# Attention scores in 32-row tiles, without a copy of the keys by head

## The chip, the cores and the metric

One core of a Trainium2 chip runs the whole kernel in one launch. The metric is the device time in microseconds of that core.

## What is computed

A two-layer decoder on x (4 sequences, 256 tokens, width 128) with a context of the same shape. After every block comes a residual add and a layer norm:

```
x = layernorm(x + self_attention_0(x))        # 16 heads of 8, rope, biases
x = layernorm(x + cross_attention_0(x, ctx))  # 16 heads of 8, biases
x = layernorm(x + mixture_0(x))               # 8 experts, all run, gate of the top 2
x = layernorm(x + causal_1(x))                # one head of width 128
x = layernorm(x + cross_attention_1(x, ctx))  # 16 heads of 8
x = layernorm(x + mixture_1(x))               # 8 experts, top 1, capacity 128
# an attention block with heads:
scores = einsum('bhqd,bhkd->bhqk', Q, K) * scale
out    = einsum('bhqk,bhkd->bhqd', softmax(scores), V) @ Wo.T + bo
```

The change touches the three blocks with 16 heads.

## The kernel before

Each sequence is a program of steps, written with `yield`. Two lanes (sequences 0, 2 and 1, 3) take turns step by step, lane 0 ahead by `LAG` = 16 steps (`take_turns`). Every engine runs the same two programs in the same turns, so the order on each engine is fixed when the kernel is built. A block with heads has a few steps of projection, 25 steps of heads (`HEAD_STEPS`), three steps at its end (`attention_end`) and three of normalisation. While one lane is in the early steps of its heads the other is in its late ones; while a lane is in the middle, the other is between two blocks. PSUM's eight banks are four pools of two, S, E, C and M, which both lanes share; `bank_turns` walks the same steps and gives each use its bank, and the helpers `wait_free`, `wait_filled` and `wait_drained` wait on the counters of that bank.

Heads have width 8. For float32r matmuls (`f32r`) Q and K are split in a high and a low part and spread out by matmuls with 0/1 matrices (`spread_rows`, L609 and L611), so that head 4t+g takes 32 partitions, 32g to 32g+31, of column block t in `q_sp` and `k_sp`. A contraction over these 32 rows gives that head's scores. Before, the contraction runs over all 128 partitions: `k_head` holds the keys of one head in its 32 partitions and zeros elsewhere. SP fills it by DMA from `k_sp`, four DMAs for each half of the heads (L543), into a buffer that POOL zeroed at the start (L460, L511); `k_sp` itself lies in the last two slots of `expo`.

One head k passes through these steps of `heads`:

- step k, PE L675: two matmuls of scores into a bank of S; DVE L1171 takes the negated maximum into `negmax`.
- four heads at a time, at step 4t+5 (`SHIFT_AT`), PE L661 transposes `negmax` into a bank of M and DVE L1166 adds it to the queries: `q_sh`.
- step k+7 (`EXP_AT`), PE L687: two matmuls of the shifted scores, keys on the partitions, into a bank of E; ACT L953 takes the exponential into one of six slots of `expo`.
- PE L703 multiplies the values of a group of four heads, each into 32 partitions of one bank of C, in two halves of the keys: the first at step 4t+11, the second at step 4t+12 (`VALUES_AT`). ACT L958 copies the bank out at step 4t+12, behind the exponential of that step. An f32 matmul is two passes on PE, so four heads are eight passes in a half.

`attention_end` transposes the contexts back (L717) when the last copy is done; DVE divides by the sums (L1182, L1183), PE transposes again (L726) and projects (L738), and the layer norm follows. The mixture (L797 to L809) uses `expo` for its hidden values.

Of the kernel before, what the change touches and what calls it, by code (L numbers as in the profile page):

```python
# [36 lines left out]
P = 128  # L37
BATCH, SEQ = 4, 256
TOKENS = BATCH * SEQ
TILES = TOKENS // P  # L40
QT = SEQ // P
# [7 lines left out]
ESLOTS = 6  # L49
# [66 lines left out]
def bank_turns():  # L116
# [4 lines left out]
    def steps(seq):  # L121
# [144 lines left out]
def decoder(nc, ins, out):  # L266
# [3 lines left out]
    with stack:  # L270
# [48 lines left out]
        def lanes(name, shape, dt=f32):  # L319
# [9 lines left out]
        k_head = lanes("k_head", [P, GROUPS, 4, SEQ], f32r)  # L329
# [40 lines left out]
        v_zeroed, lane1_zeroed = sem("v_zeroed"), sem("lane1_zeroed")  # L370
# [6 lines left out]
        k_head_ready = [[sem(f"k_head_ready{i}_{half}") for half in range(2)] for i in range(BATCH)]  # L377
# [55 lines left out]
        with nc.Block() as block:  # L433
# [25 lines left out]
            def _(pool):  # L459
                nc.gpsimd.memset(k_head[0][:].bitcast(u32), 0)  # L460
# [19 lines left out]
        with nc.Block() as block:  # L480
            @block.gpsimd
            def _(pool):
# [26 lines left out]
                nc.gpsimd.memset(v_aug[1][:].bitcast(u32), 0).then_inc(v_zeroed, 1)  # L509
                nc.gpsimd.memset(negmax[1][:].bitcast(u32), 0)  # L510
                nc.gpsimd.memset(k_head[1][:].bitcast(u32), 0)  # L511
                pool.wait_ge(v_zeroed, 2)
# [20 lines left out]
            def _(sp):  # L533
                def by_head(seq, b, what):

                    half = int(what[2])
                    wait_drained(sp, seq, b, what)
                    if seq == 1:
                        sp.wait_ge(lane1_zeroed, 1)
                    t = slice(2 * half, 2 * half + 2)  # L540
                    for g in range(4):
                        r = slice(32 * g, 32 * g + 32)
                        sp.dma_start(k_head[seq][r, t, g, :].bitcast(f32),  # L543
                                     k_sp[seq][r, t, :].bitcast(f32)
                                     ).then_inc(k_head_ready[seq][half], 16)

# [3 lines left out]
                for seq, b, what in TURNS:  # L550
                    if what in ("sk0", "sk1"):
                        by_head(seq, b, what)
                    elif b == SELF0 and seq < LANES and what[0] == "pv":
# [28 lines left out]
            def _(pe):  # L582
# [69 lines left out]

                def heads(seq, b):
                    for k in range(HEAD_STEPS):
# [10 lines left out]
                        if k < HEADS:  # L665
                            t, g = k // 4, k % 4
                            if k == 0:
                                wait_drained(pe, seq, b, "sq0")
                                pe.wait_ge(k_head_ready[seq][0], 64 * (MHA[b] + 1))
                            if k == 8:  # L670
                                wait_drained(pe, seq, b, "sq1")
                                pe.wait_ge(k_head_ready[seq][1], 64 * (MHA[b] + 1))
                            wait_free(pe, seq, b, ("max", k))
                            for qt in range(QT):
                                last = mm(where(seq, b, ("max", k))[:, qt * SEQ:(qt + 1) * SEQ],  # L675
                                          q_sp[seq][:, t, qt * P:(qt + 1) * P],
                                          k_head[seq][:, t, g, :],
                                          start=True, stop=True)
                            last.then_inc(full(seq, b, ("max", k)), 1)
                        if 0 <= k - EXP_AT < HEADS:  # L680
                            h = k - EXP_AT
                            t, g = h // 4, h % 4
                            if g == 0:
                                wait_drained(pe, seq, b, ("shift", t))
                            wait_free(pe, seq, b, ("exp", h))
                            for kt in range(QT):
                                last = mm(where(seq, b, ("exp", h))[:, kt * SEQ:(kt + 1) * SEQ],  # L687
                                          k_head[seq][:, t, g, kt * P:(kt + 1) * P],
                                          q_sh[seq][:, t, :],
                                          start=True, stop=True)  # L690
                            last.then_inc(full(seq, b, ("exp", h)), 1)
                        for kt in range(QT):
                            t = group_at(k, VALUES_AT - 1 + kt)
                            if t is None:
                                continue
                            if kt == 0:
                                wait_drained(pe, seq, b, ("exp", 4 * t + 3))
                                wait_free(pe, seq, b, ("pv", t))
                                if t == 0:
                                    wait_drained(pe, seq, b, "v")  # L700
                            for g in range(4):
                                h = 4 * t + g
                                last = mm(where(seq, b, ("pv", t))[32 * g:32 * g + 32, 0:SEQ],  # L703
# [918 lines left out]
```

## Time and profile before

| what | value |
|---|---|
| median of 3 runs | 496.33 us |
| lowest, highest | 494.31, 496.59 us |
| span of the profiled execution, first to last instruction | 492.2 us |
| PE busy | 420.9 us, 86% of the span |
| DVE busy | 311.8 us, 63% |
| ACT busy | 235.1 us, 48% |
| POOL busy | 48.6 us, 10% |
| chain that ended last | PE 64%, DVE 21%, ACT 7%, issue 4% |

The profile gives the profiled execution's span and no time of its own beside it; the three runs lie 2.1 to 4.4 us above that span. PE is TensorE's matmul, PEld its weight load, DVE VectorE, ACT ScalarE, POOL GpSimd, SP SyncE. Matmuls are pipelined: a single one of 256 columns lasts some 280 ns, but a row of them advances faster, which is why the chain of waits is the view for what a matmul costs in a stream.

### The profile page before, as it was taken

The page shows a single profiled execution, that of the slowest core. Times are in us where ns is not written, and L with a number is a line of the kernel's source. Part 1 is how long each engine was busy: PE and PEld are TensorE (multiplying, and loading weights), DVE is VectorE, ACT ScalarE, POOL GpSimd, SP SyncE. Part 2 cuts the span into 40 slices and gives each one's busy share as a digit, 9 for nine tenths or more (in the row PEclk, how much of TensorE's full clock was granted, in tenths as well). Part 3 has the DMA queues.
Part 4 walks back from the last instruction along what each step waited for, and adds up shares of the span by engine and source line. Part 5 has one row for each costly group of instructions (what it writes and reads, how often), then busy time and mean ns, then how long its engine had stood idle before and what let it go on. Part 6 is the DMA issues. An engine that isn't in the chain of part 4 may idle for free.

```text
span 492.2 us, 9126 instructions
## 1 busy us (share of the span) xinstructions
PE 420.9 (86%) x3332; PEld 340.0 (69%) x3332; DVE 311.8 (63%) x916; ACT 235.1 (48%) x527; POOL 48.6 (10%) x56
## 2 busy tenths in 40 slices
PE   3589898999999978998798989999999969984393
PEld 2476666668999966675766766668999956652292
DVE  3686766673555678685867667754755577763534
ACT  2147656663334326654255757572433437571131
POOL 6200282000000000002020000000000000010114
PEclk9889999999999999999789999999999989998588
DMA  8403323600010010002010201000010042060301
GB/s 282 142 25 89 78 72 96 161 1 1 2 31 14 2 43 1 1 3 53 1 37 16 45 1 43 1 1 2 1 43 3 1 132 82 1 182 1 95 7 34
DMA packets 18906, 22.52 MB, mean 46 GB/s; under 512 B 2984, under 2 KB 13361, under 8 KB 18864
## 3 DMA queue, kind: packets, MB, share of 16 engines
q1 hardware_dynamic: 17344, 18.68, 14.3%
q10 hardware_dynamic: 1008, 2.31, 1.4%
q0 software_dynamic: 512, 0.97, 0.6%
q8 instruction: 27, 0.44, 0.4%
q14 instruction: 15, 0.12, 0.1%
HBM read 13.63 MB, written 2.11 MB: 32 GB/s over the span
## 4 chain that ended last, share of the span: by engine, by line
PE 64%; DVE 21%; ACT 7%; issue 4%; DMA 1%; SPq 0%; POOLq 0%; POOL 0%; DVEq 0%; ACTq 0%
PE bank_C L809 12%; PE bank_S L675 8%; PE bank_C L703 7%; PE bank_E L687 7%; DVE negmax L1171 5%; PE bank_M L609 3%; ACT expo L953 2%; PE bank_M L738 2%; PE bank_M L611 2%; PE bank_E L797 2%; PE bank_S L797 2%; PE bank_M L661 2%; PE bank_E L799 2%; PE bank_E L798 2%; DVE x_rows L1219 1%
## 5 line engine op out<-in xcount | busy, mean ns | idle before, releaser
L1171 DVE TENSOR_REDUCE negmax<-bank_S 128x2 f32<-128x512 f32 x192 | 128.4, 685 | 50.3 <-PE bank_S L675 50.1
L953 ACT ACTIVATE expo<-bank_E 128x512 f32<-128x512 f32 x192 | 113.5, 597 | 83.5 <-PE bank_E L687 82.3
L675 PE MATMUL bank_S<-k_head,q_sp 128*128 128x256 f32 x384 | 97.0, 338 | 10.7 <-DVE negmax L1171 7.2
L675 PEld LDWEIGHTS bank_S<-k_head,q_sp 128*128 128x128 f32 x384 | 61.5, 199 | 39.1 <-issue 25.0
L687 PE MATMUL bank_E<-q_sh,k_head 128*128 128x256 f32 x384 | 81.3, 294 | 0.7 <-DVE q_sh L1166 0.5
L703 PE MATMUL bank_C<-expo,v_aug 128*32 128x256 f32 x768 | 61.5, 393 | 4.6 <-ACT expo L953 4.6
L687 PEld LDWEIGHTS bank_E<-q_sh,k_head 128*128 128x128 f32 x384 | 60.3, 194 | 6.5 <-issue 3.5
L809 PE MATMUL bank_C<-mix_w,expo 128*128 128x128 f32 x512 | 62.5, 275 | 0.7 <-issue 0.7
L809 PEld LDWEIGHTS bank_C<-mix_w,expo 128*128 128x128 f32 x512 | 59.9, 192 | 1.1 <-issue 1.1
L1014 ACT ACTIVATE expo<-bank_S,b 128x256 f32<-128x256 f32 x64 | 26.8, 470 | 53.6 <-PE bank_S L799 53.2
L1276 DVE TENSOR_SCALAR expo<-bank_E,b 128x256 f32<-128x256 f32 x64 | 27.9, 477 | 28.1 <-PE bank_E L799 28.0
L486 POOL TENSOR_TENSOR xb<-x_rows,rows 128x256 f32<-128x256 f32 x12 | 8.4, 706 | 320.6 <-DVE x_rows L1219 318.1
L1287 DVE SCALAR_TENSOR_TENSOR y<-bank_C,g_w,y 128x128 f32<-128x128 f32 x64 | 19.4, 345 | 25.3 <-PE bank_C L809 25.3
L609 PE MATMUL bank_M<-qk_hi,spread 128*128 128x256 f32 x96 | 26.3, 306 | 10.4 <-DVE qk_lo L1110 5.3
L609 PEld LDWEIGHTS bank_M<-qk_hi,spread 128*128 128x128 f32 x96 | 18.1, 188 | 16.4 <-DVE qk_lo L1110 10.7
L703 PEld LDWEIGHTS bank_C<-expo,v_aug 128*32 128x32 f32 x768 | 15.2, 108 | 18.3 <-ACT expo L953 6.6
L912 ACT ACTIVATE expo<-bank_M,const 128x512 fp32r<-128x512 f32 x24 | 15.4, 684 | 19.4 <-PE bank_M L611 19.4
L611 PE MATMUL bank_M<-qk_lo,spread 128*128 128x256 f32 x96 | 24.1, 281 | 0.0
L661 PE MATMUL bank_M<-const,negmax 128*128 128x128 f32 x96 | 20.0, 291 | 1.5 <-DVE ctx_n L1183 1.3
L797 PE MATMUL bank_S<-qk_hi,w_hi 128*128 128x256 f32 x64 | 20.6, 322 | 0.0
L1166 DVE TENSOR_TENSOR q_sh<-q_sp,bank_M 128x256 fp32r<-128x256 f32 x48 | 19.8, 413 | 1.0 <-PE bank_M L661 1.0
L958 ACT ACTIVATE ctx_sb<-bank_C 128x256 f32<-128x256 f32 x48 | 18.6, 387 | 3.9 <-PE bank_C L703 3.8
(185 smaller groups left out, 654.7 us busy)
## 6 DMA issues: line engine op xcount, KB each, us to landing
k_head<-expo SPq DMA_DIRECT2D x96, 64.0 KB, 2.0
mix_w<-in_mix_w SPq DMA_DIRECT2D x24, 256.0 KB, 3.3
expo<-in_mix_w SPq DMA_DIRECT2D x6, 256.0 KB, 6.1
proj_w<-in_proj ACTq DMA_DIRECT2D x1, 640.0 KB, 11.5
xe_scratch<-empty_row SPq DMA_DIRECT2D x1, 520.0 KB, 6.1
expo<-xe_scratch SPq DMA_DIRECT2D x2, 260.0 KB, 3.1
expo<-in_spread SPq DMA_DIRECT2D x1, 512.0 KB, 7.9
expo<-in_spread ACTq DMA_DIRECT2D x1, 512.0 KB, 8.5
```

The lines of the kernel that those rows point to most:

```text
L609: mm(dst, spread[:, hi, t, :], qk_hi[seq][:, i, :], start=True, stop=False)
L611: last = mm(dst, spread[:, lo, t, :], qk_lo[seq][:, i, :], start=False, stop=True)
L661: last = nc.tensor.transpose(where(seq, b, ("shift", t))[:, qt * P:(qt + 1) * P], negmax[seq][:, t, qt, :], ident)
L675: last = mm(where(seq, b, ("max", k))[:, qt * SEQ:(qt + 1) * SEQ], q_sp[seq][:, t, qt * P:(qt + 1) * P], k_head[seq][:, t, g, :], start=Tr ...
L687: last = mm(where(seq, b, ("exp", h))[:, kt * SEQ:(kt + 1) * SEQ], k_head[seq][:, t, g, kt * P:(kt + 1) * P], q_sh[seq][:, t, :], start=Tr ...
L703: last = mm(where(seq, b, ("pv", t))[32 * g:32 * g + 32, 0:SEQ], v_aug[seq][:, kt, h, :], expo[seq][:, h % ESLOTS, kt * SEQ:(kt + 1) * SEQ ...
L797: mm(dst, w_hi, hi, start=True, stop=False)
L809: last = mm(where(seq, b, ("down", e))[:, qt * P:(qt + 1) * P], hidden[:, (e % 2) * FC + f, qt * P:(qt + 1) * P], mix_w2[:, e, f, :], star ...
L953: activate(expo[seq][:, h % ESLOTS, :], where(seq, b, ("exp", h))[:], ACT.Exp, scale=scale).then_inc(free(seq, b, ("exp", h)), 1)
L1014: last = activate(hidden[:, (e % 2) * FC + f, :], where(seq, b, ("up", n))[:, i * SEQ:(i + 1) * SEQ], ACT.Relu, bias=b1[:, e * FC + f:e * ...
L1171: V.tensor_reduce(negmax[seq][:, k // 4, :, 32 * (k % 4)], where(seq, b, ("max", k))[:].rearrange("p (q n) -> p q n", q=QT), AX.X, ALU.max ...
L1276: last = V.tensor_scalar(hidden[:, (e % 2) * FC + f, :], where(seq, b, ("up", n))[:, i * SEQ:(i + 1) * SEQ], b1[:, e * FC + f:e * FC + f + ...
```

## The change

It removes `k_head`, its 96 DMAs and its semaphores. `k_sp` gets a buffer of its own and `expo` has eight slots. The scores read `q_sp` and `k_sp` (and the shifted scores `q_sh` and `k_sp`) on the 32 partitions of the head alone. The two matmuls of scores and the two of shifted scores of one step are issued alternately, after the waits of both. Both halves of a group's values come in step 4t+12, and ACT copies them out in step 4t+13; the last group's copy is the first thing of `attention_end`.

```diff
-ESLOTS = 6
+ESLOTS = 8
...
-                if group_at(k, VALUES_AT - 1) is not None:
-                    turn(b, ("pv", group_at(k, VALUES_AT - 1)), "C")
+                if group_at(k, VALUES_AT) is not None:
+                    turn(b, ("pv", group_at(k, VALUES_AT)), "C")
...
-        k_head = lanes("k_head", [P, GROUPS, 4, SEQ], f32r)
+        k_sp = lanes("k_sp", [P, GROUPS, SEQ], f32r)
...
-        k_sp = [e[:, ESLOTS - 2:ESLOTS, :].rearrange("p a (t n) -> p (a t) n", n=SEQ).bitcast(f32r)
-                for e in expo]
...
-                nc.gpsimd.memset(k_head[0][:].bitcast(u32), 0)
+                nc.gpsimd.memset(v_aug[1][:].bitcast(u32), 0).then_inc(v1_zeroed, 1)
+                nc.gpsimd.memset(negmax[1][:].bitcast(u32), 0)
...
-                def by_head(seq, b, what):
-
-                    half = int(what[2])
-                    wait_drained(sp, seq, b, what)
-                    if seq == 1:
-                        sp.wait_ge(lane1_zeroed, 1)
-                    t = slice(2 * half, 2 * half + 2)
-                    for g in range(4):
-                        r = slice(32 * g, 32 * g + 32)
-                        sp.dma_start(k_head[seq][r, t, g, :].bitcast(f32),
-                                     k_sp[seq][r, t, :].bitcast(f32)
-                                     ).then_inc(k_head_ready[seq][half], 16)
...
+                def score(seq, b, h, qt):
+
+                    t, g = h // 4, slice(32 * (h % 4), 32 * (h % 4) + 32)
+                    return mm(where(seq, b, ("max", h))[:, qt * SEQ:(qt + 1) * SEQ],
+                              q_sp[seq][g, t, qt * P:(qt + 1) * P], k_sp[seq][g, t, :],
+                              start=True, stop=True)
+
+                def shifted_score(seq, b, h, kt):
+
+                    t, g = h // 4, slice(32 * (h % 4), 32 * (h % 4) + 32)
+                    return mm(where(seq, b, ("exp", h))[:, kt * SEQ:(kt + 1) * SEQ],
+                              k_sp[seq][g, t, kt * P:(kt + 1) * P], q_sh[seq][g, t, :],
+                              start=True, stop=True)
...
                             wait_free(pe, seq, b, ("max", k))
-                            for qt in range(QT):
-                                last = mm(where(seq, b, ("max", k))[:, qt * SEQ:(qt + 1) * SEQ],
-                                          q_sp[seq][:, t, qt * P:(qt + 1) * P],
-                                          k_head[seq][:, t, g, :],
-                                          start=True, stop=True)
-                            last.then_inc(full(seq, b, ("max", k)), 1)
                         if 0 <= k - EXP_AT < HEADS:
                             h = k - EXP_AT
-                            t, g = h // 4, h % 4
-                            if g == 0:
-                                wait_drained(pe, seq, b, ("shift", t))
+                            if h % 4 == 0:
+                                wait_drained(pe, seq, b, ("shift", h // 4))
                             wait_free(pe, seq, b, ("exp", h))
+                        for half in range(2):
+                            if k < HEADS:
+                                last = score(seq, b, k, half)
+                                if half == 1:
+                                    last.then_inc(full(seq, b, ("max", k)), 1)
+                            if 0 <= k - EXP_AT < HEADS:
+                                h = k - EXP_AT
+                                last = shifted_score(seq, b, h, half)
+                                if half == 1:
+                                    last.then_inc(full(seq, b, ("exp", h)), 1)
+                        t = group_at(k, VALUES_AT)
+                        if t is not None:
+                            wait_drained(pe, seq, b, ("exp", 4 * t + 3))
+                            wait_free(pe, seq, b, ("pv", t))
...
-                        if group_at(k, VALUES_AT) is not None:
-                            t = group_at(k, VALUES_AT)
-                            wait_filled(act, seq, b, ("pv", t))
-                            activate(ctx_sb[seq][:, t, :], where(seq, b, ("pv", t))[:, 0:SEQ],
-                                     ACT.Copy).then_inc(free(seq, b, ("pv", t)), 1)
+                        if group_at(k, VALUES_AT + 1) is not None:
+                            context(seq, b, group_at(k, VALUES_AT + 1))
                         yield
...
                 def attention_end(seq, b, side):
+                    context(seq, b, GROUPS - 1)
                     next(side, None)
                     yield
```

The order on PE while lane 1 is in the middle of its heads and lane 0 between the first and the second attention block. Before: L738 is lane 0's output projection, L749 its transpose of x; L675 and L687 are the two kinds of scores of lane 1, L703 its values, L661 its shift.

```order
L738 MATMUL bank_M<-proj_w,aT 128x128
L675 MATMUL bank_S<-k_head,q_sp 128x256 [waits drained_S1]
L675 MATMUL bank_S<-k_head,q_sp 128x256
L687 MATMUL bank_E<-q_sh,k_head 128x256 [waits drained_E0,drained_M0]
L687 MATMUL bank_E<-q_sh,k_head 128x256
L703 MATMUL bank_C<-expo,v_aug 32x256 [waits drained_C0,drained_C1,drained_E1]
L703 MATMUL bank_C<-expo,v_aug 32x256 x3
L675 MATMUL bank_S<-k_head,q_sp 128x256 [waits drained_S0]
L675 MATMUL bank_S<-k_head,q_sp 128x256
L687 MATMUL bank_E<-q_sh,k_head 128x256 [waits drained_E1]
L687 MATMUL bank_E<-q_sh,k_head 128x256
L703 MATMUL bank_C<-expo,v_aug 32x256 x4
```

The same place with the change (L724 was L738; L635 and L642 are the two kinds of scores, L690 the values):

```order
L724 MATMUL bank_M<-proj_w,aT 128x128
L635 MATMUL bank_S<-k_sp,q_sp 128x256 [waits drained_E0,drained_M0,drained_S1]
L642 MATMUL bank_E<-q_sh,k_sp 128x256
L635 MATMUL bank_S<-k_sp,q_sp 128x256
L642 MATMUL bank_E<-q_sh,k_sp 128x256
L635 MATMUL bank_S<-k_sp,q_sp 128x256 [waits drained_E1,drained_S0]
L642 MATMUL bank_E<-q_sh,k_sp 128x256
L635 MATMUL bank_S<-k_sp,q_sp 128x256
L642 MATMUL bank_E<-q_sh,k_sp 128x256
L690 MATMUL bank_C<-expo,v_aug 32x256 [waits drained_C0,drained_C1,drained_E1]
L690 MATMUL bank_C<-expo,v_aug 32x256 x7
```

The two visits to the values are one, one step later, and each step's four score matmuls alternate between S and E behind one set of waits.

ACT at the end of lane 0's heads, before: L953 are exponentials (of both lanes), L958 the copy of lane 0's last group of values, L903 and L905 the next block's keys.

```order
L953 ACTIVATE expo<-bank_E 128x512 [waits filled_E0]
L958 ACTIVATE ctx_sb<-bank_C 128x256 [waits filled_C1]
L953 ACTIVATE expo<-bank_E 128x512 [waits filled_E1]
L903 ACTIVATE qk_hi<-bank_M,cols 128x256 [waits filled_M1]
L905 ACTIVATE qk<-bank_M,cols 128x256
```

With the change (L939 exponentials, L947 the copy, L889 and L891 the keys):

```order
L939 ACTIVATE expo<-bank_E 128x512 [waits filled_E0]
L939 ACTIVATE expo<-bank_E 128x512 [waits filled_E1]
L947 ACTIVATE ctx_sb<-bank_C 128x256 [waits filled_C1]
L889 ACTIVATE qk_hi<-bank_M,cols 128x256 [waits filled_M1]
L891 ACTIVATE qk<-bank_M,cols 128x256
```

The last copy of a block now stands behind one more exponential, that of the other lane. On PE the back transposes wait for that copy in both kernels.

## Rows read from the trace of the kernel before

**Rows 1.** The page, parts 1 and 2: busy time, and the granted clock in 40 slices

```profile
PE 420.9 (86%) x3332; PEld 340.0 (69%) x3332; DVE 311.8 (63%) x916; ACT 235.1 (48%) x527; POOL 48.6 (10%) x56
...
PEclk9889999999999999999789999999999989998588
```

**Rows 2.** Groups of instructions: busy us, mean ns of one | idle before, releaser

```profile
L1171 DVE TENSOR_REDUCE negmax<-bank_S 128x2 f32<-128x512 f32 x192 | 128.4, 685 | 50.3 <-PE bank_S L675 50.1
L953 ACT ACTIVATE expo<-bank_E 128x512 f32<-128x512 f32 x192 | 113.5, 597 | 83.5 <-PE bank_E L687 82.3
L675 PE MATMUL bank_S<-k_head,q_sp 128*128 128x256 f32 x384 | 97.0, 338 | 10.7 <-DVE negmax L1171 7.2
...
L687 PE MATMUL bank_E<-q_sh,k_head 128*128 128x256 f32 x384 | 81.3, 294 | 0.7 <-DVE q_sh L1166 0.5
L703 PE MATMUL bank_C<-expo,v_aug 128*32 128x256 f32 x768 | 61.5, 393 | 4.6 <-ACT expo L953 4.6
L687 PEld LDWEIGHTS bank_E<-q_sh,k_head 128*128 128x128 f32 x384 | 60.3, 194 | 6.5 <-issue 3.5
...
L1166 DVE TENSOR_TENSOR q_sh<-q_sp,bank_M 128x256 fp32r<-128x256 f32 x48 | 19.8, 413 | 1.0 <-PE bank_M L661 1.0
L958 ACT ACTIVATE ctx_sb<-bank_C 128x256 f32<-128x256 f32 x48 | 18.6, 387 | 3.9 <-PE bank_C L703 3.8
```

**Rows 3.** Busy time in three stretches: length, engines, granted clock, DMA share, GB/s

```profile
63.71:71.60 7.89, 7.56 (x67) 5.07 (x67) 5.82 (x10) 5.00 (x10) 7.56 (x9) 1.00 0.23 69
71.60:86.30 14.70, 12.94 (x102) 10.02 (x102) 10.18 (x28) 9.65 (x22) 3.46 (x4) 1.00 0.40 104
106.00:180.00 74.00, 71.51 (x602) 66.68 (x601) 40.05 (x138) 29.36 (x78) 0.69 (x1) 1.00 0.05 11
```

**Rows 4.** The chain of waits, 63.7 to 72.3 us: start, length, what

```profile
63.71 0.43 PE bank_S L675 x2
...
66.43 0.43 PE bank_S L675 x2
...
67.10 0.57 PE bank_C L703 x8
...
68.34 0.22 PE bank_M L661 x2
68.56 0.24 PE bank_S L675 x2
...
69.07 0.61 ACT expo L953
...
69.72 0.64 PE bank_C L703 x8
...
72.26 0.51 PE bank_M L717 x4
```

**Rows 5.** The chain of waits in the first mixture, 139 to 170 us

```profile
139.17 1.78 PE bank_C L809 x16
140.95 0.64 PE bank_M L777 x4
141.59 0.32 PE bank_M L609
...
169.88 0.45 PE bank_M L589 x2
```

**Rows 6.** The chain of waits between two attention blocks of lane 0

```profile
77.59 0.24 PE bank_S L675 x2
77.83 0.23 PE bank_E L687 x2
```

**Rows 7.** The start: two rows of the chain, and one of ACT's timeline

```profile
17.59 2.03 DMA k_head<-expo
...
19.76 0.49 PE bank_S L675 x2
...
16.75 1.08 ACT L920 ACTIVATE q_sp<-bank_M 128x512 fp32r<-128x512 f32 x2 [0.64 <-PE bank_M L611]
```

More of the change, by code:

```diff
@@ L375, in decoder @@
         drained = {pool: [sem(f"drained_{pool}{i}") for i in range(n)] for pool, n in POOLS.items()}
-        k_head_ready = [[sem(f"k_head_ready{i}_{half}") for half in range(2)] for i in range(BATCH)]
         split_q_ready = [sem(f"split_q_ready{i}") for i in range(BATCH)]
@@ L507, in scatter @@
                         ).then_inc(scattered, 16)
[L509 to L512, printed above, removed]
+                pool.wait_ge(v1_zeroed, 1)
                 nc.gpsimd.memset(v_aug[1][:, :, :, HD:HD + 1], 1.0).then_inc(lane1_zeroed, 1)
@@ L550, in _ @@
                 for seq, b, what in TURNS:
-                    if what in ("sk0", "sk1"):
-                        by_head(seq, b, what)
-                    elif b == SELF0 and seq < LANES and what[0] == "pv":
+                    if b == SELF0 and seq < LANES and what[0] == "pv":
                         wait_filled(sp, seq, b, what)
@@ L681, in heads @@
                             h = k - EXP_AT
-                            t, g = h // 4, h % 4
-                            if g == 0:
-                                wait_drained(pe, seq, b, ("shift", t))
+                            if h % 4 == 0:
+                                wait_drained(pe, seq, b, ("shift", h // 4))
                             wait_free(pe, seq, b, ("exp", h))
-                            for kt in range(QT):
[L687 to L703, printed above, removed]
-                                          v_aug[seq][:, kt, h, :],
-                                          expo[seq][:, h % ESLOTS, kt * SEQ:(kt + 1) * SEQ],
-                                          start=(kt == 0), stop=(kt == QT - 1))
-                            if kt == QT - 1:
-                                last.then_inc(full(seq, b, ("pv", t)), 1)
+                        for half in range(2):
[8 more added lines that the diff above has]
+                                    last.then_inc(full(seq, b, ("exp", h)), 1)
@@ new lines, in heads @@
+                        t = group_at(k, VALUES_AT)
+                        if t is not None:
+                            wait_drained(pe, seq, b, ("exp", 4 * t + 3))
+                            wait_free(pe, seq, b, ("pv", t))
+                            if t == 0:
+                                wait_drained(pe, seq, b, "v")
+                            for kt in range(QT):
+                                for g in range(4):
+                                    h = 4 * t + g
+                                    last = mm(where(seq, b, ("pv", t))[32 * g:32 * g + 32, 0:SEQ],
+                                              v_aug[seq][:, kt, h, :],
+                                              expo[seq][:, h % ESLOTS, kt * SEQ:(kt + 1) * SEQ],
+                                              start=(kt == 0), stop=(kt == QT - 1))
+                            last.then_inc(full(seq, b, ("pv", t)), 1)
@@ L954, in heads, with context @@
                                      ACT.Exp, scale=scale).then_inc(free(seq, b, ("exp", h)), 1)
-                        if group_at(k, VALUES_AT) is not None:
-                            t = group_at(k, VALUES_AT)
-                            wait_filled(act, seq, b, ("pv", t))
-                            activate(ctx_sb[seq][:, t, :], where(seq, b, ("pv", t))[:, 0:SEQ],
-                                     ACT.Copy).then_inc(free(seq, b, ("pv", t)), 1)
+                        if group_at(k, VALUES_AT + 1) is not None:
+                            context(seq, b, group_at(k, VALUES_AT + 1))
                         yield
+                def context(seq, b, t):
+                    wait_filled(act, seq, b, ("pv", t))
+                    activate(ctx_sb[seq][:, t, :], where(seq, b, ("pv", t))[:, 0:SEQ],
+                             ACT.Copy).then_inc(free(seq, b, ("pv", t)), 1)
                 def attention_end(seq, b, side):
+                    context(seq, b, GROUPS - 1)
                     next(side, None)
```

7 lines of the change are left out of this document (3 added, 4 removed).

## Prediction, made before the change was run

> **What bounds the kernel now.** I read the page first, then the groups of instructions, then the busy time by stretch, and last the chain of waits in the stretches that the change touches. The page says PE is busy 420.9 of 492.2 us and DVE 311.8, at full granted clock in most slices [rows 1]. So PE is the first suspect, but 14% of the span is free of it and 37% of DVE's. The groups [rows 2] give the price of one head's pass: two matmuls of scores (S), one DVE maximum of 685 ns, two matmuls of shifted scores (E), one ACT exponential of 597 ns. The stretches [rows 3] show three situations. (a) 63.71 to 71.60: one lane is in its last exponentials and values (V), the other in its first scores. PE is busy 7.56 of 7.89 us. (b) 71.60 to 86.30: one lane has both S and E in each step, the other goes from one attention block to the next. PE is busy 12.94 of 14.70 us, less than in (a). (c) 106 to 180: the first mixture, PE 71.51 of 74 us. In the chain, (a) is PE almost without a break [rows 4]; a pair of S costs 0.24 us where nothing of another shape stands before it, 0.43 us right behind V. The same 0.19 us shows behind another change of shape: four L777 passes (8 partitions of contraction) take 0.64 us behind L809, whose passes cost 1.78/16 = 0.11, so 0.64 - 0.45 = 0.19 to get in, and the first L609 pass behind it takes 0.32 instead of 0.12, 0.20 to get out [rows 5]. The work of L777 is no more than L809's, so the rest is the change of the array's shape. This is the row on which I rest most.
>
> The rule behind it: the Trainium skill, TensorEngine Tiling (Array Packing), Key Properties, says that changing the tiling mode, though not the tile within a mode, drains TensorE. The trace agrees, with 0.19 and 0.20 us.
>
> **The change, part by part**, with its sum for one execution.
>
> *Changes of shape.* V is a 32-column shape and all else but L777 is full. Before, the PE order has 95 runs of V, hence 190 changes, at 0.13 into V and 0.19 out some 30 us. After, S and E have a 32-row shape of their own: I count 134 changes full to row, 114 row to full, 46 row to V, 26 V to row, 24 between V and full, 344 in all. At 0.13 into V and 0.19 to 0.20 otherwise these are some 64 us, 33 more than before, if none hides. The 0.13: a visit of two rounds takes 0.57 [rows 4]; a 256-column f32 pass is 0.45/2 = 0.22 [rows 5], so 0.13 is entry.
>
> *Values in one step.* Two visits of 0.57 + 0.19 = 0.76 become one of 4 x 0.22 + 0.13 + 0.19 = 1.20, which saves 0.32 us for each of 48 groups. V also stands two steps behind its last exponential instead of one, so the 0.61 us that the chain spends on the exponential before V at 69.07 [rows 4] goes.
>
> *Score tiles.* Before, S S E E of a step cost 4 x 0.12 = 0.47 us. After, the order is S E S E, S on one quarter of the rows and E on the next, into different banks. No row of this trace has two row tiles in flight, so the price is bounded: 0.24 if the two quarters run side by side, 0.47 if they take turns. I take 0.24, since the four V matmuls of a round, on four column quarters, do run side by side (eight in 0.57 us where one alone is 0.22). At lane boundaries (E E then S S) the neighbours are on different quarters too.
>
> *(a), eight such stretches in the order.* From 63.71 to the back transposes at 72.26 is 8.55 us [rows 4]. Up to 69.05 (5.34 us) PE would need 6 x 0.24 + one V 1.20 + two shifts of 0.22 + 0.39 = 3.9 us, but DVE has five maxima and two shifts of q, 5 x 0.685 + 2 x 0.41 = 4.25 [rows 2], so DVE is late next: 4.45 with its gaps. From 69.05 on (3.21 us): S E 0.24, V 0.13 + 0.88, S E 0.43, then the new wait. ACT now copies the last context at the start of the attention end, behind the other lane's exponential, and PE's back transposes are queued behind that copy, with the whole of PE behind them: 0.60 + 0.39 [rows 2] and some 0.10 of handing over. Sum 2.77. So 8.55 becomes 7.2; I take a gain of 1.2 each to leave room for DVE running dry during the 1.20 us of V: **-9.6 us**.
>
> *(b), twelve turnovers.* Here PE mostly waits on a chain through ACT and DVE of the other lane, so neither the halved S E nor most of the new changes count. What stands in the chain is an S E pair between two full-shape steps, as at 77.59 and 77.83 [rows 6]: 0.47 becomes 0.24 + 0.39 = 0.63. With one to three such places in a turnover, +0.3 each, **+3.6 us**.
>
> *(c), mixtures and ragged ends.* Lone pairs E E or S S stand between full-shape steps; nothing overlaps in them and each costs 0.39 more. The order has 43 lone pairs, 16 of them inside (a). Of the other 27 some 14 lie in the two mixtures, where PE is saturated: 14 x 0.39 = 5.5, less four merged V visits of 0.32, is 4.2; the others mostly wait anyway, 0.8. **+5.0 us**.
>
> *The copy of keys.* 96 DMAs leave SP. Only the first is in the chain: S starts at 19.76 because the DMA lands then [rows 7]. The q copies on ACT start at 16.75 and the first half is done 0.54 later; with a change of shape S could start near 17.6: **-2.2 us**. The loads of mixture weights behind those DMAs on SP wait for V and move with it; they were never waited for on PE.
>
> *Edits at no cost.* Eight exp slots (h >= 8 waits for V instead of h >= 6) only loosen ACT. S now also waits for its partner E's bank and for the shift; ACT frees E two turns ahead, cover 0.60 against a step of about 1.0 (7.89/8); if ACT were late, the maximum would be late by the same. The POOL memsets shrink in the first block, hidden by the loads; the k_sp buffer of its own costs nothing.
>
> Sum: -9.6 + 3.6 + 5.0 - 2.2 = -3.2. The profiled execution has a span of 492.2, so 489.0; the median of the three runs is 4.1 above that span, so 496.3 - 3.2, about **493 us**. A difference of 0.5% (2.5 us) is about what a measurement can tell from none.
>
> **Rivals.** *No side by side (20%).* The two quarters take turns, 0.47 stays, and every change of shape is a loss. (a) gives back all but 0.1 each: -1. (b) three places of +0.39 each: 12 x 1.1 = +13. (c) +5, start -2. About 511 us, slower. It decides as soon as an S E S E costs over some 0.35 us. For it: each load of 128 columns takes 194 ns [rows 2] and pairs already stand 0.12 apart, the pace of loads as much as of matmuls. Against it: the V rounds. The Trainium skill, TensorE: Matmul & The Clock Gate, Part 3, says that a load overlaps a running matmul only in another row group; by that rule S0's successor on its own quarter is exposed and the quartet stays near 0.47, this rival. In the full shape the trace differs: pairs 0.12 apart hide loads behind matmuls on the same rows. The same page measures 3.07 times for four row tiles, which speaks for overlap; no run here shows that.
>
> *The changes hide (15%).* Most fall where PE waits in any case, or are shorter between row tiles than at L777. Then (b) is -3, (c) +1, (a) -9.6, start -2.2: about 483 us. For it: the 1.8 us in which PE is free in (b) [rows 3].
>
> *The clock falls (10%).* PE is granted half the clock in a few slices, after light stretches [rows 1]. Drains make PE lighter; if 10 to 20 us of work in heads ran at half speed, it would take as much again: 505 to 515.
>
> **How the numbers follow.** My case has 55%, by itself 487 to 500. Of it 0.31 is faster, 0.16 within 0.5%, 0.08 slower. The hidden case adds 0.14 to faster and 0.01 to the same, the other two 0.30 to slower. The range 483 to 511 reaches to both other cases and leaves out the clock's tail and values below 483.
>
> **What would show it.** Right: four S E matmuls between others in about 0.24 us, L609 or L738 behind a row pair 0.19 later than before, one V run of 16 passes per group at 1.0 us, DVE gaps shrinking in (a), a new PE wait for ctx_sb at the back transposes of about 1 us, the first S near 17.6. Wrong: S E S E at 0.47, changes of 0.05, or half the granted clock in slices where it is full now.

## The result, and the profile after

| | before | after |
|---|---|---|
| median, us | 495.94 (494.31 to 496.59, 4 runs) | 588.3 (581.46 to 591.7, 4 runs) |
| ratio to before | | 1.1775, 95% interval 1.1718 to 1.1832 |
| profiled run, us | span 492.2 | 585.86, span 584.1 |
| mean granted clock of TensorE | 0.954 | 0.733 |

The change makes the kernel 92 us slower by the medians; runs of one kernel differ in the clock that they were granted (0.723 to 0.740 in these four), and by the two faster ones alone, from which the ratio is taken, it is 88 us. The forecast was 493, with a range of 483 to 511: the time lies far outside it, and on the other side of no change.

The page of the changed kernel, parts 1 and 2. They answer to [rows 1]:

```profile
PE 510.8 (87%) x3332; PEld 371.8 (64%) x3332; DVE 316.9 (54%) x916; ACT 232.3 (40%) x527; POOL 41.3 (7%) x54
...
PEclk9686659656999955555768958557999975655578
```

PE does the same 3332 matmuls in 510.8 us instead of 420.9. The clock row says why: each digit is the mean of one slice, a 9 is at or near full speed (2.4 GHz) and a 5 is half (1.2 GHz). Of the 40 digits 25 are now 5 to 7, where before it was two and all others were 8 or 9. At only two levels, a mean of 0.733 over 584.1 us is 2 x 0.267 x 584.1 = 312 us at half the clock; before it was 2 x 0.046 x 492.2 = 45 us.

The groups of the changed kernel (busy us, mean ns of one | idle before, releaser). They answer to [rows 2]; L635 are the scores, L642 the shifted scores, L690 the values:

```profile
L1160 DVE TENSOR_REDUCE negmax<-bank_S 128x2 f32<-128x512 f32 x192 | 129.6, 687 | 95.8 <-PE bank_S L635 95.5
L939 ACT ACTIVATE expo<-bank_E 128x512 f32<-128x512 f32 x192 | 113.6, 597 | 164.8 <-PE bank_E L642 163.1
L635 PE MATMUL bank_S<-k_sp,q_sp 32*128 32x256 f32 x384 | 115.5, 412 | 11.2 <-DVE negmax L1160 10.8
L642 PE MATMUL bank_E<-q_sh,k_sp 32*128 32x256 f32 x384 | 113.1, 431 | 3.5 <-ACT expo L939 3.2
...
L690 PE MATMUL bank_C<-expo,v_aug 128*32 128x256 f32 x768 | 78.7, 550 | 1.9 <-ACT expo L939 1.9
```

DVE and ACT cost per instruction what they did (687 and 597 ns). They only wait longer for PE: the idle time of the maxima behind L635 went from 50.1 to 95.5 us, that of the exponentials from 82.3 to 163.1. PE alone slowed down, its value matmuls as well (550 ns against 393, means over both levels of the clock), whose shape the change leaves alone. So the loss is not only a price of the score matmuls themselves.

Busy time by stretch (columns as in [rows 3]), in four stretches of the changed kernel:

```profile
63.70:87.50 23.80, 21.67 (x119) 13.85 (x120) 10.29 (x22) 8.49 (x17) 12.41 (x13) 0.50 0.21 67
87.50:108.00 20.50, 17.22 (x155) 10.50 (x154) 13.48 (x30) 13.96 (x30) 0.68 (x1) 1.00 0.38 92
108.00:142.20 34.20, 33.79 (x167) 23.92 (x168) 14.07 (x42) 12.38 (x30) 0.00 (x0) 0.50 0.00 1
142.20:207.00 64.80, 61.88 (x516) 58.79 (x514) 37.02 (x128) 23.35 (x64) 0.69 (x1) 1.00 0.00 1
```

The stretches at 0.50 are attention heads; 142 to 207 us is the first mixture, whose matmuls are of the full shape, at 1.00. Note the busy share where the clock is low: 21.67 of 23.80 us is 91%, and 33.79 of 34.20 is 99%. From 87.5 to 108 us, at full clock, it is lower, 17.22 of 20.50 or 84%. The profile, in which the ends of matmuls are modelled, calls PE busy at 0.50, and it stays at half the clock all the same. The Trainium skill, TensorE: Matmul & The Clock Gate, Part 1, says that the clock is set by how busy PE has lately been. The profile's busy share here does not bear that out.

At full clock the changed order can be read without that disturbance. The chain of waits of the changed kernel, 88.8 to 108.6 us, nearly all of it at full clock (start, length, what):

```profile
88.89 0.31 PE bank_S L635
89.20 0.00 PE bank_E L642
89.20 0.11 PE bank_S L635
89.32 0.00 PE bank_E L642
89.32 0.66 PE bank_M L724 x4
...
97.47 0.43 PE bank_E L642 x2
97.90 1.00 PE bank_C L690 x16
...
103.54 0.40 DVE negmax L1160
103.94 0.21 issue
104.15 0.41 DVE q_sh L1155
104.56 0.62 DVE negmax L1160
...
107.22 0.60 ACT expo L939
107.81 0.28 ACT ctx_sb L947
108.10 0.04 issue
108.14 0.47 PE bank_M L703
```

The E matmuls add nothing beside S: the two quarters run side by side, and the four from 88.89 on take 0.43 us with 0.19 for the change of shape, as forecast. The second S, on the same quarter as the first, stands 0.11 us behind it. Sixteen V passes take 1.00 us. Two things are new in the chain. DVE's work stands in it in a row (maximum, shift of q, maximum: 1.64 us, with 0.21 of issue), and the last context copy stands behind an exponential just ahead of the back transposes.

The start, in the chain of waits of the changed kernel (it answers to [rows 7]):

```profile
15.57 0.61 ACT q_sp L906
...
16.23 0.51 PE bank_S L635 x3
```

S starts 3.5 us earlier than at 19.76; the forecast was 2.2. The wait for the copy of the keys gives 2.35 of it: S stood 3.01 us behind the start of the q copy (19.76 - 16.75) and now stands 0.66 behind it. The other 1.2 us were not forecast: the q copy itself starts at 15.57 instead of 16.75. Two rows of the timeline before, and one of the changed kernel, show where they come from:

```profile
9.74 3.52 POOL L511 MEMSET k_head<- 128x4096 uint32 x1
11.73 1.68 DVE L1145 CAST qk_hi<-qk 128x256 fp32r<-128x256 f32 x1
...
11.93 0.29 DVE L1134 CAST qk_hi<-qk 128x256 fp32r<-128x256 f32 x1
```

DVE's first cast took 1.68 us while POOL zeroed `k_head`, and 0.29 in the change, which has no such memset. In the runs below it is 1.95 and 1.68 with the memset (runs 1 and 7) and 0.29 without (runs 2 and 9). No run takes out this memset alone.

### The profile page after: what moved, and what is told of

It reads as the page before. It is cut to its first block, busy times and chain, and to the rows that moved or that the text cites. A ratio compares the mean times of both kernels' runs of the same rounds, so it can differ in the third digit from the quotient of the medians.

```text
span 584.1 us, 9071 instructions
## 1 busy us (share of the span) xinstructions
PE 510.8 (87%) x3332; PEld 371.8 (64%) x3332; DVE 316.9 (54%) x916; ACT 232.3 (40%) x527; POOL 41.3 (7%) x54
## 2 busy tenths in 40 slices
DMA packets 11226, 16.23 MB, mean 28 GB/s; under 512 B 1448, under 2 KB 5681, under 8 KB 11184
## 4 chain that ended last, share of the span: by engine, by line
PE 79%; DVE 10%; ACT 5%; issue 3%; DMA 1%; POOL 0%; POOLq 0%; DVEq 0%; ACTq 0%
PE bank_S L635 13%; PE bank_C L690 12%; PE bank_C L795 10%; PE bank_E L642 5%; PE bank_M L654 4%; PE bank_M L703 4%; DVE negmax L1160 3%; PE bank_M L588 3%; ACT expo L939 3%; PE bank_M L724 2%; PE bank_M L590 2%; PE bank_E L783 2%; PE bank_M L568 2%; PE bank_S L783 2%; PE bank_E L784 1%
## 5 line engine op out<-in xcount | busy, mean ns | idle before, releaser
L1160 DVE TENSOR_REDUCE negmax<-bank_S 128x2 f32<-128x512 f32 x192 | 129.6, 687 | 95.8 <-PE bank_S L635 95.5
L939 ACT ACTIVATE expo<-bank_E 128x512 f32<-128x512 f32 x192 | 113.6, 597 | 164.8 <-PE bank_E L642 163.1
L635 PE MATMUL bank_S<-k_sp,q_sp 32*128 32x256 f32 x384 | 115.5, 412 | 11.2 <-DVE negmax L1160 10.8
L642 PE MATMUL bank_E<-q_sh,k_sp 32*128 32x256 f32 x384 | 113.1, 431 | 3.5 <-ACT expo L939 3.2
L635 PEld LDWEIGHTS bank_S<-k_sp,q_sp 32*128 32x128 f32 x384 | 73.5, 250 | 60.6 <-issue 38.2
L642 PEld LDWEIGHTS bank_E<-q_sh,k_sp 32*128 32x128 f32 x384 | 70.4, 260 | 15.8 <-issue 9.2
L690 PE MATMUL bank_C<-expo,v_aug 128*32 128x256 f32 x768 | 78.7, 550 | 1.9 <-ACT expo L939 1.9
L690 PEld LDWEIGHTS bank_C<-expo,v_aug 128*32 128x32 f32 x768 | 25.7, 142 | 28.6 <-issue 21.2
L703 PE MATMUL bank_M<-const,ctx_sb 128*128 128x128 f32 x96 | 20.8, 389 | 8.5 <-ACT ctx_sb L947 8.5
L703 PEld LDWEIGHTS bank_M<-const,ctx_sb 128*128 128x128 f32 x96 | 16.8, 203 | 11.8 <-ACT ctx_sb L947 11.8
L654 PEld LDWEIGHTS bank_M<-const,negmax 128*128 128x128 f32 x96 | 13.9, 190 | 14.4 <-issue 13.2
L898 ACT ACTIVATE k_sp<-bank_M,const 128x512 fp32r<-128x512 f32 x24 | 15.4, 686 | 17.0 <-PE bank_M L590 16.8
```

The costliest lines, as they stand in the source:

```text
L635: return mm(where(seq, b, ("max", h))[:, qt * SEQ:(qt + 1) * SEQ], q_sp[seq][g, t, qt * P:(qt + 1) * P], k_sp[seq][g, t, :], start=True, s ...
L642: return mm(where(seq, b, ("exp", h))[:, kt * SEQ:(kt + 1) * SEQ], k_sp[seq][g, t, kt * P:(kt + 1) * P], q_sh[seq][g, t, :], start=True, s ...
L654: last = nc.tensor.transpose(where(seq, b, ("shift", t))[:, qt * P:(qt + 1) * P], negmax[seq][:, t, qt, :], ident)
L703: last = nc.tensor.transpose(where(seq, b, f"back{qt}")[:, t * P:(t + 1) * P], ctx_sb[seq][:, t, qt * P:(qt + 1) * P], ident)
L939: activate(expo[seq][:, h % ESLOTS, :], where(seq, b, ("exp", h))[:], ACT.Exp, scale=scale).then_inc(free(seq, b, ("exp", h)), 1)
L1160: V.tensor_reduce(negmax[seq][:, k // 4, :, 32 * (k % 4)], where(seq, b, ("max", k))[:].rearrange("p (q n) -> p q n", q=QT), AX.X, ALU.max ...
```

## The experiments

Theory A: the granted clock falls when the score matmuls are made of small row tiles, and that is nearly the whole loss. Rivals: it falls by the new order or the later values (B); or by the more frequent changes of shape (A2). The first two runs cut the change in two: all of it but the tiles, and the tiles alone.

**1. The whole change, but scores over all 128 rows.** The keys are copied by head with DMAs as before, in six slots; the mixed order, V in one step and the late copies are kept.

```diff
-ESLOTS = 8
+ESLOTS = 6
-  q_sp[seq][g, t, qt * P:(qt + 1) * P], k_sp[seq][g, t, :],
+  q_sp[seq][:, t, qt * P:(qt + 1) * P], k_head[seq][:, t, h % 4, :],
```

> The whole change but for the tiles: S and E contract over 128 partitions again, from keys by head copied by DMA, with six exp slots; the order S E S E, the merged values and the late copy stay. Theory A (the 32-row tiles lower the granted clock): mean clock 0.93 or more and 480 to 500 us. Theory B (the new order, waits and merged values let PE run dry, and the clock falls for that): mean clock below 0.85 and over 540 us.

Measured: 506.09 us (504.71 to 509.54), ratio 1.0196 (1.016 to 1.0232); before on the same chip 496.16. The clock is as theory A has it, the time lies above the 480 to 500 that I expected.

**2. The kernel before with 32-row tiles alone**, in its old order S S E E, V in two steps.

```diff
-  q_sp[seq][:, t, qt * P:(qt + 1) * P],
-  k_head[seq][:, t, g, :],
+  q_sp[seq][32 * g:32 * g + 32, t, qt * P:(qt + 1) * P],
+  k_sp[seq][32 * g:32 * g + 32, t, :],
```

> The kernel before with the 32-row tiles alone: S S E E in order, waits, values in two visits, copy and six slots as before, no copy of keys. Theory A: mean clock 0.70 to 0.80 and 560 to 600 us. Theory B: mean clock 0.93 or more and 495 to 515 us, longer than before by the changes of shape alone.

Measured: 587.09 us (572.2 to 590.4). The clock rows of the page, of run 1:

```profile
PEclk9589999999999989998789999999999989995588
```

and of run 2:

```profile
PEclk9686996558999855555555878966999955655578
```

Mean clocks of these executions: 0.932 and 0.730. By the medians the tiles alone give 91 of the 92 us, all the rest together gives 10. B is out for the clock. The runs of run 2 spread widely (572.2 us at a clock of 0.759 to 590.4 at 0.724), so a difference of some 10 us between it and the change can't be read. That the change alternates S and E and run 2 does not shows in no time (588.3 against 587.09), and the chain of waits of run 2 says why:

```profile
71.15 0.31 PE bank_S L655
71.46 0.01 PE bank_E L667
71.47 0.11 PE bank_S L655
71.58 0.06 PE bank_E L667
```

The kernel issues S S E E there, and each E still starts beside an S on the other quarter, as it does again from 72.94 us on. Side by side does not need the new order.

**3 and 4. The kernel before with V in one step**, one step later. In run 3 all context copies come a step later too, the last at the start of the attention end, as in the change. In run 4 that last copy stays in the last head step:

```diff
+                        if k == HEAD_STEPS - 1:
+                            context(seq, b, GROUPS - 1)
                         yield
...
                 def attention_end(seq, b, side):
-                    context(seq, b, GROUPS - 1)
```

> The kernel before with the merged values and the late copy alone, scores over 128 rows in the order S S E E. Both theories keep the clock if only tiles matter (A): 0.94 or more. A: -0.32 us for 48 groups and no wait before the values, +1.0 at 12 block ends, so 485 to 495 us. B: below 0.9 and over 505 us.

> As the run with merged values and late copy, but the last group's copy stays in the last step of the heads, ahead of the other lane's exponential. If the late last copy costs about 1.0 us at each of 12 block ends, this one is 8 to 12 us faster than that run; if its wait lies beside other work, the two agree within 2 us.

Measured: 506.87 us (502.57 to 507.09), ratio 1.0181 (1.0124 to 1.0238), and 499.78 us (497.18 to 500.85), ratio 1.0063 (1.0039 to 1.0087). Run 3 is above the 485 to 495 that I expected. Run 1, which differs from run 3 in the order of S and E and of the waits ahead of them, has 506.09: the order alone is worth nothing that shows. The late last copy costs 7.1 us, a little under the 8 to 12 expected. V in one step brings nothing, where I had counted on it as the larger part of the gain in (a). Run 4 is 3.6 us slower than the kernel before, but its clock is also lower, 0.930 to 0.951 against 0.944 to 0.965; its three runs at 0.940 and 0.941 took 497.2, 497.7 and 499.4 us and those of the kernel before at 0.944 took 496.8 to 497.7, so much of the 3.6 may be the clock's. One such stretch at full clock shows why there is no gain. The chain of waits in the kernel before:

```profile
86.29 0.23 PE bank_E L687 x2
86.52 0.57 PE bank_C L703 x8
...
92.47 0.61 ACT expo L953
...
95.67 0.27 PE bank_M L717 x2
```

The same work in run 4:

```profile
87.38 0.24 PE bank_E L687 x2
...
91.50 1.00 PE bank_C L701 x16
92.50 0.45 PE bank_S L675 x2
...
92.97 0.48 DVE negmax L1172
93.45 0.12 issue
93.58 0.41 DVE q_sh L1167
93.99 0.61 DVE negmax L1172
94.60 0.04 issue
94.64 0.51 PE bank_S L675 x2
...
97.06 0.50 PE bank_M L714 x4
```

From the first E to the back transposes it was 95.67 - 86.29 = 9.38 us and is 97.06 - 87.38 = 9.68. The exponential of 0.61 us is gone from the chain, as forecast, but during the 1.00 us of V DVE gets no new scores, and then its maximum, the shift of q and the next maximum come one after another with PE waiting. One wait has taken the place of the other. In the change itself the same stretch is 108.14 - 97.47 = 10.67, the late copy included.

**5. Run 1 with 64-row tiles**, two heads at a time, one of them against zeros:

```diff
-  q_sp[seq][:, t, ...], k_head[seq][:, t, h % 4, :],
+  q_sp[seq][g, t, ...], k_head[seq][g, t, h % 2, :],     # g: 64 rows
```

> As the run over 128 rows, but S and E contract over 64-row tiles that hold two heads, one of them against zeros (keys copied by DMA). As many changes of shape as in the changed kernel, twice as many rows of the array at work in a score matmul, S and E side by side only where their halves differ. Theory A1 (the clock follows how much of the array is at work): mean clock between 0.78 and 0.92 and 515 to 560 us. Theory A2 (the clock falls for the many changes of shape and the gaps they leave): as in the changed kernel, 0.70 to 0.76 and 570 to 600 us.

Measured: 563.39 us (546.93 to 571.08), the clocks 0.807 to 0.861. The clock row:

```profile
PEclk9769998555999995899569999977999976975588
```

With the same order, copies and number of matmuls the mean clock is 0.932, 0.841 and, in the change, 0.733 for tiles of 128, 64 and 32 rows. The clock lies in the range of A1, and the median time just above its 515 to 560. Three quarters of the rows that run 1 multiplies hold zeros in the keys, as in the kernel before, and its clock is 0.932 all the same: in this kernel rows of zeros did not bring the clock down.

**6. The kernel before with one short 32-row matmul ahead of S in 108 head steps**, which adds 216 changes of shape and no work that is used.

```diff
+                            if k >= EXP_AT:
+                                mm(where(seq, b, ("max", k))[:, 0:P], q_sp[seq][0:32, t, 0:P],
+                                   k_head[seq][0:32, t, 0, 0:P], start=True, stop=True)
```

> The kernel before, with one short matmul of 32 rows ahead of the full-shape S in the 108 steps that have both S and E: 216 changes of shape more than before, the scores themselves over 128 rows. It computes nothing new (its result is overwritten). Theory A1: mean clock 0.92 or more, and at most 216 x 0.19 + 108 x 0.1 = 52 us longer, less what waits hide: 515 to 545 us. Theory A2: mean clock below 0.85 and over 550 us.

Measured: 523.48 us (520.74 to 533.93), ratio 1.0516 (1.0483 to 1.0549), before 495.89. The clock row:

```profile
PEclk9569999999999985799959999999999999999588
```

216 changes, more than the some 150 that the change adds, leave the clock at 0.919 (its other runs 0.940 to 0.947): A2 is out as the cause. By the ratio they cost 25.6 us in the end time, 0.12 each with the short matmul included, less than the 0.19 that a change takes on PE, so some of it seems to lie in time that PE waits anyway.

**7. 32-row tiles in the first five heads of the first sequence only**, where the DMA copy of the keys is in the chain. The spread keys of that half lie in `q_sh` for that time; all else is as before.

```diff
+FIRST = 5
...
+                            first = (seq, b) == (0, SELF0) and k < FIRST
+                                r = slice(32 * g, 32 * g + 32) if first else slice(0, P)
```

> The kernel before, in which only the first five heads of the first sequence take their S from 32-row tiles, so that the start does not wait for the DMA copy of the keys; all else as before. In the changed kernel the first S stood at 16.2 us instead of 19.8. If the tiles cost only where much of the time is spent in them: 2 to 4 us faster than before, 492 to 494 us, mean clock as before. If the slower start of the lane is taken up later anyway, or even five heads lower the clock for long: no faster.

Measured: 493.5 us (492.63 to 495.74), ratio 0.9953 (0.9936 to 0.997), before 495.89. The mean clock is 0.954. This version is 2.4 us faster than the kernel before.

**8 and 9. The changed kernel with tiles in one of three attention blocks, and in none.** A block without tiles contracts over all 128 rows of k_sp. These rows hold four heads, so the separate scores of the heads are left out there, and the exponential's scale is set to 1e-6; order, slots and copies are those of the change:

```diff
+RAW = (CROSS0, CROSS1)          # run 9: (SELF0, CROSS0, CROSS1)
...
+                    if b in RAW:
+                        g = slice(0, P)
...
-                    scale = float(HD) ** -0.5
+                    scale = 1e-6 if b in RAW else float(HD) ** -0.5
```

> The changed kernel, with 32-row score tiles only in the first of the three attention blocks (the self-attention of the first sequence's stretch). The two cross-attention blocks contract S and E over all 128 rows of the k_sp block, which sums the scores of four heads, with an exponential's scale of 1e-6: the separate scores of the heads are left out there, and the output isn't the reference's. Order, instruction counts, slots and copies stay those of the change. Theory A (the granted clock follows how much of the array the score matmuls use): half clock only in the stretches of the one block that keeps tiles, about a third of the loss; mean granted clock 0.86 to 0.90, time 520 to 545 us. Rival B (the clock falls by the order, the merged values or the eight slots): clock stays at about 0.73 and the time at 580 to 590 us.

> The changed kernel with all three attention blocks contracting S and E over all 128 rows of the k_sp block, scale 1e-6: separate scores of heads are left out everywhere, and the output isn't the reference's; no copy of keys by head, eight slots, order and values as in the change. Theory A: granted clock 0.93 or more in the mean, 498 to 508 us (506.1 of the run with 128-row scores and copies, less up to 4 us for the start without a copy). Rival B (something else in the change, such as reading k_sp and q_sp directly without the copy, or eight slots, holds the clock low): clock under 0.85, time over 535 us.

Measured: run 8 516.32 us (512.25 to 518.28), ratio 1.0399 (1.0324 to 1.0474), clock 0.909; run 9 498.48 us (496.62 to 499.5), ratio 1.0037 (1.0016 to 1.0058), clock 0.955; before 496.32. Busy time by stretch in run 8, where 39 to 63 us are heads of the block that keeps tiles, and 63.7 to 87.5 are mostly heads of a block without:

```profile
39.00:63.00 24.00, 20.92 (x138) 12.95 (x138) 13.90 (x35) 12.57 (x29) 2.61 (x4) 0.72 0.12 37
...
63.70:87.50 23.80, 21.28 (x161) 15.23 (x162) 13.37 (x32) 12.44 (x25) 12.34 (x13) 0.93 0.21 67
```

In the changed kernel the same 63.7 to 87.5 us stood at 0.50. So the tiles account for 588.3 - 498.5 = 90 us, and the clock follows them block by block. The data of the scores differ in these runs too, but run 1 holds its clock with the true scores. One block of three gives 18 us, a fifth, and both the time and the clock came out milder than I had expected (520 to 545 us, 0.86 to 0.90). The trace of the change itself accounts for that: its S matmuls of the first block stand from 16.23 to 62.59 and from 277.99 to 330.30 us, at 0.74 and 0.77, which is 24 + 24 = 48 us at half clock out of its 312. The same two stretches of run 8 have 0.74 and 0.75, some 51 us. The first block never held a third of the half clock; five sixths of it lie elsewhere, in and between the stretches of the other two.

The chain of waits in run 9, four scores over 128 rows in a row:

```profile
92.97 0.32 PE bank_S L638
93.28 0.12 PE bank_E L647
93.40 0.12 PE bank_S L638
93.52 0.13 PE bank_E L647
```

Here each E takes its 0.12 us; in the tiles of the change it added 0.00 to 0.01.

**10 and 11. The late copy by itself.** Run 10 is the kernel before with only the last context copy moved to the attention end:

```diff
-                        if group_at(k, VALUES_AT) is not None:
+                        if group_at(k, VALUES_AT) is not None and k < HEAD_STEPS - 1:
...
                 def attention_end(seq, b, side):
+                    context(seq, b, GROUPS - 1)
```

Run 11 is run 9 with that copy back in the last head step, by the same edit as between runs 3 and 4.

> The kernel before with one edit: the last of a block's four context copies is issued at the start of the attention end instead of in the last head step, so behind the other lane's exponential; everything else as before. Theory (the late copy is what costs in the late-values run against the mixed one, 7.1 us): 501 to 505 us. Rival (the late copy only hurts together with the values in one step, which end later): 495 to 499 us.

> The run without row tiles (all scores over 128 rows of k_sp, scale 1e-6, separate scores of heads left out, so the output isn't the reference's), with the last context copy back in the last head step. Theory (the late copy costs some 7 us in any kernel at full clock): 490 to 493 us, under the kernel before by about the start's gain and a little of term (a). Rival (the late copy costs nothing here, where the copy of the keys is gone and the order of scores is mixed): 497 to 500 us.

Measured: run 10 505.05 us (503.17 to 507.3), ratio 1.0181 (1.0147 to 1.0216), clock 0.951; run 11 491.29 us (488.7 to 493.21), ratio 0.9899 (0.9863 to 0.9935); before 495.9. PE's waits in run 10 (us in total, times, longest):

```profile
PE bank_M L717 <- ACT ctx_sb L961: 8.2, 9, 1.0
```

One instruction moved behind another on ACT, in 12 places, costs 9.2 us alone and some 7 us in the full change without tiles (498.48 - 491.29). Nine of the waits show, at about 0.9 us each. Run 11 says what the rest of the change is worth with neither tiles nor late copy: 4.6 us. The separate scores of the heads are missing in it, so it is a bound and not a kernel to keep.

## Why the prediction was wrong

**The clock.** This is the step that failed. The sum has no term for the clock: it prices every part at the full clock of the kernel before and so puts what the tiles do to it at nothing. Measured was a mean of 0.733 in place of 0.954. Only the rival "The clock falls", at 10%, had it, with 10 to 20 us of head work at half speed, caused by drains that make PE lighter, for 505 to 515 us (493 with as much again is 503 to 513). Its mechanism was the wrong one too, and its amount small by more than ten times. What did hold is the sign that the prediction named: half the granted clock in slices where it was full. Runs 2, 5, 8 and 9 show that the tiles bring it, and run 6 that the changes of shape do not. Against run 9 the change spends 312 - 45 = 267 us more at half clock (profiled run 585.86 against 498.5 us, so 87.4 us lost), which is 0.33 us lost per us. In run 8 it is 93 - 45 = 48 us for 16.4, or 0.34, and in run 2 316 - 45 = 271 us for 91, or 0.34. "As much again" would be 0.5 us lost per us of the slower kernel; a third was measured here. That DVE and ACT do not slow with PE (687 and 597 ns) is a likely reason, not a tested one. With the 64-row tiles it was more: run 5 against run 1 has 176 - 69 = 107 us more at half clock for 554.4 - 507.4 = 47 us of span, 0.44. [Rows 1] had shown one slice at half clock, and I read that as a property of light stretches. I never asked what it would make of score matmuls that leave three quarters of the rows idle.

**Side by side.** Right: four tiles cost what two full passes do. It gained nothing even so, because at half the clock two passes side by side last about as long as four before. It does not hang on the alternating order either, as run 2 shows. The rival "No side by side" (20%, 511 us) is refuted in its mechanism.

**Changes of shape.** Right in price: 0.19 us in the chain, and about 0.12 each in the end time. Their sum in the change can't be seen beside the loss.

**Stretch (a), -9.6 us.** Wrong. (PE's own time in it is 1.44 + 1.20 + 0.44 + 0.39 = 3.5, not 3.9; DVE's 4.45 decided, so nothing hangs on it.) I saw that DVE would be late next and put it at 4.45 us for its own work, as if that work could be spread evenly; the 0.15 us that I left for DVE running dry were too few. It can't: V in one step leaves DVE without scores for 1.00 us and then it has three instructions to do with PE behind them (run 4). And the late copy was in my sum, at some 1.1 us for each of eight stretches, but taken from a gain that was not there; it acts at all 12 attention ends and costs 7.2 to 9.2 us. At full clock a stretch of this kind is 10.67 us against 9.38, +1.3 where I had -1.2.

**(b) and (c), +8.6 us**, are not separated by any run. Run 9 has no row tiles and so none of their changes, and it stands at +2.2 us. By an estimate of its parts that is +7.2 for the late copy, -3.5 or so for the start and -1.5 for all the rest.

**The start, -2.2 us.** Right in sign and mechanism, with 2.35 us for the wait on the copy. The other 1.2 us of the 3.5 come from the shorter cast on DVE, which I had not seen. Run 7, with tiles at the start only and the memset still there, is 2.4 us faster in the end time.

**Edits at no cost.** Eight slots, no copies and fewer memsets were put at nothing. For the memset of `k_head` that was wrong: the cast beside it is 1.4 us shorter without it. Runs 1 and 9 differ by these, the start and the data in the keys' idle rows, and are 7.6 us apart. The start gives some 4 of it (first S at 20.16 and 16.15 us in their chains); from 20 to 62 us the granted clock is 0.89 in run 1 and 1.00 in run 9, which may be the rest. This was not tried apart.

**Open:** what the chip counts when it lowers the clock. The runs show that it goes with the rows of the score tiles and not with the order, the changes of shape, the zeros or the profile's busy share. They don't tell whether it is the idle rows of a pass or that side by side tiles finish the same work in less array time: no run has row tiles throughout that do not run side by side, since in the old order S S E E they do so as well (run 2), and in part in run 5.

## What to carry to other kernels

Contracting over 128 rows with three quarters of them zeros looks like waste, and here it held PE at full clock: look at the granted clock before the busy share whenever an edit makes tiles smaller, and try one block first. Where a fused step saves time on one engine, ask what the engine behind it does meanwhile and what it then has to do in a row. A copy that another engine's queue waits for should stand ahead of work that nobody waits for; one exponential ahead of it cost 7 to 9 us here.

## What was not expected of the hardware

- Score tiles of 128, 64 and 32 rows gave a mean granted clock of 0.932, 0.841 and 0.733 (runs 1 and 5 and the change), with PE 91 and 99% busy in two stretches of the change at half clock.
- At half clock all of PE slows, whatever the shape: 393 to 550 ns in the mean for the untouched V matmuls. Each us at half clock was a third of a us lost, by runs 2 and 8 and the change, and 0.44 by run 5.
- Two row tiles into different banks run side by side without a trace in the chain: 0.00 to 0.01 us for the second, against 0.12 over 128 rows, and also where both of one quarter are issued before both of the other (run 2).
- DVE's cast of 128x256 from f32 to fp32r took 1.68 to 1.95 us beside POOL's memset of `k_head`, and 0.29 without it.
